# Three more waits between the four gathers of a group in a graph network's edge loop

## The reference

```python
h = x @ W1 + b1
m = relu(concat([h[dst], h[src] - h[dst]]) @ W2 + b2)
m = relu(m @ W3 + b3)
x = layernorm(x + relu(segment_max(m, dst)))
msgs = edge_weight[:, None] * x[src]
x = layernorm(x + segment_sum(msgs, dst) @ W.T + b)
```

## Time and profile before

| what | value |
|---|---|
| median of 3 runs | 2713.13 us (2711.83 to 2724.68) |
| the profiled execution | 2716.54 us, its span 2714.8 us |
| mean granted clock of TensorE | 0.880 |
| PE, DVE, POOL, ACT busy in the span | 2111.0, 1614.8, 1355.9, 824.2 us |
| DMA queue of POOL (q0) | 53312 packets, 138.17 MB |
| gathers of q rows | 784, 827.7 us busy on POOL, 478.4 us idle before them |

### The profile page before, as it was taken

One profiled execution on the slowest core, in us unless ns is written; L12 is line 12 of the kernel. 1 busy time (PEld: TensorE's weight loads), 2 busy tenths in 40 slices (PEclk: granted clock), 3 DMA queues, 4 the chain that ended last, 5 costly groups with the idle time before them and its releaser, 6 DMA issues.

```text
span 2714.8 us, 61794 instructions
## 1 busy us (share of the span) xinstructions
PE 2111.0 (78%) x15960; PEld 1850.6 (68%) x15960; DVE 1614.8 (59%) x4239; ACT 824.2 (30%) x2385; POOL 1355.9 (50%) x1300
## 2 busy tenths in 40 slices
PE   5526877777777777777785289999999999889995
PEld 5425656556565555555563289898989888888885
DVE  3326666666666666666679444443444444789997
ACT  1222223223233232232232144444545445000003
POOL 6435666666666666666634335555556555100000
PEclk7767888888888888888887599999999999999998
DMA  3224555555555555555552166666666666788885
GB/s 111 84 79 128 145 146 141 143 147 142 137 144 141 142 147 142 144 144 144 144 140 79 27 191 206 203 203 210 201 202 208 207 204 208 234 252 247 251 252 171
DMA packets 534340, 447.34 MB, mean 165 GB/s; under 512 B 64731, under 2 KB 499383, under 8 KB 534240
## 3 DMA queue, kind: packets, MB, share of 16 engines
q1 hardware_dynamic: 342788, 208.10, 28.0%
q0 software_dynamic: 53312, 138.17, 16.3%
q10 hardware_dynamic: 138140, 100.06, 12.7%
HBM read 300.43 MB, written 145.64 MB: 164 GB/s over the span
## 4 chain that ended last, share of the span: by engine, by line
PE 61%; another core or an unknown queue 17%; issue 10%; DVE 5%; ACT 3%; DVEq 2%; POOL 1%; DMA 1%; SPq 0%; ACTq 0%; POOLq 0%
PE z_ps L1426 10%; PE t_ps L1426 10%; PE z_ps L1351 6%; PE m_ps L1339 6%; PE z_ps L1450 5%; PE m_ps L1338 5%; PE m_ps L1450 4%; PE s_ps L1414 3%; PE t_ps L1360 3%; PE t_ps L1450 2%; PE s_ps L1318 1%; POOL whole L420 1%; PE s_ps L1317 1%; DVEq L1156 1%
## 5 line engine op out<-in xcount | busy, mean ns | idle before, releaser
L414 POOL DMA_INDIRECT whole<-q_tab,src_ti x784 | 827.7, 1056 | 478.4 <-issue 197.2
L430 POOL DMA_INDIRECT tab<-whole,row_at x392 | 420.3, 1072 | 373.7 <-ACT whole L688 183.2
L1097 DVE TENSOR_SCALAR whole<-row_bc,node_id 128x768 f32<-128x768 uint8 x392 | 229.7, 627 | 366.8 <-remote 123.9
L1338 PE MATMUL m_ps<-ident,whole 128*128 128x128 f32 x1568 | 337.3, 300 | 19.1 <-DMA win<-p_tab 12.6
L1339 PE MATMUL m_ps<-oh,win 128*128 128x128 f32 x1568 | 328.5, 293 | 4.4 <-issue 4.1
L1426 PE MATMUL t_ps<-win,whole 128*128 128x128 f32 x2352 | 305.3, 286 | 21.3 <-issue 17.2
L1426 PE MATMUL z_ps<-win,whole 128*128 128x128 f32 x2352 | 300.6, 284 | 19.9 <-issue 8.6
L1426 PEld LDWEIGHTS t_ps<-win,whole 128*128 128x128 f32 x2352 | 282.7, 197 | 26.7 <-issue 20.6
L1145 DVE SCALAR_TENSOR_TENSOR whole<-iota_f,scratch,whole 128x384 f32<-128x384 f32 x440 | 269.5, 613 | 45.9 <-PE m_ps L1450 34.8
L1426 PEld LDWEIGHTS z_ps<-win,whole 128*128 128x128 f32 x2352 | 278.6, 195 | 26.2 <-issue 20.0
L1338 PEld LDWEIGHTS m_ps<-ident,whole 128*128 128x128 f32 x1568 | 272.9, 218 | 21.1 <-issue 21.0
(11 more groups left out here) (270 smaller groups left out, 3104.3 us busy)
## 6 DMA issues: line engine op xcount, KB each, us to landing
win<-p_tab SPq DMA_DIRECT2D x784, 64.0 KB
seg_tab<-run_e ACTq DMA_DIRECT2D x196, 256.0 KB
win<-xw_tab SPq DMA_DIRECT2D x784, 64.0 KB
whole<-tab SPq DMA_DIRECT2D x220, 200.0 KB
whole<-tab ACTq DMA_DIRECT2D x220, 200.0 KB
row_bc<-seg_row_tab SPq DMA_DIRECT2D x196, 128.0 KB
row_bc<-rel_tab SPq DMA_DIRECT2D x196, 96.0 KB
whole<-q_tab,src_ti POOLq DMA_INDIRECT x784
```

The lines of the kernel that those rows point to most:

```text
L414: pool.indirect_dma_start(qg[:, g % RING, j, :], None, q_tab[:, :], IOA(ap=src_ti[:, t:t + 1], axis=0)).then_inc(q_ld[g % RING], 16)
L430: pool.indirect_dma_start(tab[:, :], IOA(ap=row_at[0:FR, k:k + 1], axis=0), fat[0:FR, k % RR, :], None).then_inc(fat_st[k % RR], 16)
L1097: last = V.tensor_scalar(pick[:, s, j, :], row_bc[:, r, 0:GK * SLOTS], node_id[:, j:j + 1], None, ALU.is_equal)
L1338: mm(m1_ps[:, s, c], lhsT=qg[:, r % RING, j, :], rhs=ident[:], start=True, stop=False)
```

## The change

For groups from RING + 2 = 14 on, the second, third and fourth gather of a group each wait for an event of their own: first_done of group g-11 (POOL waits for the count g - RING + 2), run_ev of group g-14 (count g - RING - 1), and run_done of group g-13 (count g - RING). The first gather waits for m1_done as before.

```diff
@@ -411,6 +411,13 @@
                     pool.wait_ge(m1_done, g - RING + 1)
                 for j in range(GT):
                     t = GT * g + j
+                    if g >= RING + 2:
+                        if j == 1:
+                            pool.wait_ge(first_done, g - RING + 2)
+                        if j == 2:
+                            pool.wait_ge(run_ev, g - RING - 1)
+                        if j == 3:
+                            pool.wait_ge(run_done, g - RING)
                     pool.indirect_dma_start(qg[:, g % RING, j, :], None, q_tab[:, :], IOA(ap=src_ti[:, t:t + 1], axis=0)).then_inc(q_ld[g % RING], 16)
```

## The result

| | before | after |
|---|---|---|
| median | 2712.48 us (2710.0 to 2724.68, 4 runs) | 2755.52 us (2746.58 to 2764.83, 4 runs) |
| ratio | | 1.0151 [1.012, 1.0182] |
| profiled execution | 2716.54 us | 2761.03 us, its span 2759.3 us |

The forecast was 2640 us, a gain of 73; it became a loss of 43, outside the range of 2560 to 2730. Lines behind the change stand seven higher in the kernel after: L414 is L421, L625 L632, L900 L907, L942 L949. In the kernels of the experiments they are shifted by each one's own edit (by three in most: L900 is L903 there, L942 L945, L973 L976).

What follows compares the result with a forecast made beforehand. The prediction took PE's signals, held while gathers are under way, to bound the first edge loop at 6.43 us a group. Spacing would save 0.41 x 182 = 75 us from 2716.5, giving 2641, stated as 2640 us; range 2560 to 2730.

Steps and rivals of the forecast that it cites:

- What bounds the loop: First edge loop: something that goes with the gathers costs 2.2 us a group, over 400 us in all.
- The rival by which nothing matters but bytes on shared DMA engines: First edge loop: events already passed or bytes under way set the hold-up, so nothing changes, 2713 us; chance 0.16.
- That PE's signal is held while gathers are under way: First edge loop: PE's signals pass before a train's data or after its last landing; waiters released 2.2 us late.
- 4 x 1.25 + 1.3 = 6.3 us: Period of a group in the first edge loop: four gather steps of 1.25 us plus 1.3 until the last has landed.
- POOL's floor: POOL's gathers in the first edge loop need 21.6 us in four groups against 25.7, a ceiling of 187 us gained.
- I take 1.65 us in four groups, 40% of it: Gain from spacing gathers in the first edge loop: 40% of the 4.1 us ceiling, 0.41 x 182 = 75 us.
- the term of 75 us: Gain expected from spaced gathers over 182 groups of the first edge loop: 0.41 us each, 75 us.
- the sign that the prediction named for this case: If right, ACT's wait before L625 would be shorter than the 1.6 us seen over one train.
- The held gather: Beside DVE's one-hot L942: gather 1, now waiting for L900, loses its 1.56 us overlap but waits as long; nothing either way.
- Rival 2: First edge loop: POOL becomes the efficient bound at 21.6 us in four groups, 2526 us; chance 0.07.
- Rival 1: First edge loop: run_ev's held signal delays gathers 2 and 3 by 1.7 us, losing 62 us, 2775 us; chance 0.22.

Runs made afterwards that it cites:

- no_gathers: Kernel before with gathers for the first 12 groups only, the rest reading the ring's old rows; 2297.21 us, ratio 0.847.
- tiny_rows: Kernel before with each gather from group 12 on fetching 4 bytes of its 128 rows instead of 512; 2708.87 us, ratio 0.9982.
- plain_loads: Kernel before with every gather of q rows replaced by a plain DMA of 128 consecutive rows, issued by SP; 2409.17 us, ratio 0.8881.
- half_gathers: Kernel before with only the first two gathers of each group issued from group 12 on; 2301.33 us, ratio 0.8601.
- spaced: Kernel before with a small iota on POOL behind each of a group's first three gathers; 2722.62 us, ratio 1.0035.
- pairs: Changed kernel with only the third gather waiting, for first_done, and no other new wait; 2714.98 us, ratio 1.001.
- w1_first: Changed kernel with only the second gather's new wait (first_done) kept; 2761.93 us, ratio 1.0178.
- w23_late: Changed kernel without the second gather's wait, keeping the third's for run_ev and the fourth's for run_done; 2734.47 us, ratio 1.007.
- w1_turn_again: Kernel before plus the second gather's wait for first_done only where g is a multiple of four (the large one-hot's step); 2786.04 us, ratio 1.0267.
- w1_turn: Kernel before plus the second gather's wait for first_done only where g is a multiple of four, batch with before at 2346.03 us; 2344.92 us, ratio 1.0.
- w1_rest: Kernel before plus the second gather's wait for first_done only where g isn't a multiple of four, batch with before at 2346.03 us; 2346.46 us, ratio 1.0.
- w3_only: Changed kernel with only the fourth gather's wait, for run_done, batch with before at 2346.03 us; 2344.24 us, ratio 0.9993.
- after_rest: Changed kernel with its three waits dropped where g is a multiple of four, batch with before at 2346.03 us; 2346.93 us, ratio 1.0002.
- two_groups: Kernel before with POOL waiting for m1_done only once for two groups, so trains of eight gathers; 2932.14 us, ratio 1.0807.
- w1_rest_again: Kernel before plus the second gather's wait for first_done only where g isn't a multiple of four; 2731.25 us, ratio 1.0076.
- after_rest_again: Changed kernel with its three waits dropped where g is a multiple of four; 2705.59 us, ratio 1.0124, in the batch with before at 2675.68 us.

## Why the prediction was wrong

**What bounds the loop** was right in the main. It was to be the gathers, at 2.2 us a group and over 400 us; no_gathers gives 415 and 4.14 us a group. That q rows aren't late, that the bytes don't count, that the tail keeps its pace and that all stages behind 1420 us stay: each was found so. The rival by which nothing matters but bytes on shared DMA engines falls with tiny_rows and plain_loads: more than a quarter of the moved bytes taken away (143 to 103 GB/s) changed 0.2% of the time. The Trainium skill (DMA: Bandwidth & Descriptors, "Issuing engines are not separate DMA queues") says that DMAs started by any engine run on the same 16 DMA engines and interleave there; nothing here speaks against that, but it prices no part of this loop.

That PE's signal is held while gathers are under way was read from one train and holds for the loop. The table gives the mean time from the end of a group's last matmul of `gathered` (or from the end of ACT's operation before, where that is later) until ACT starts relu_1, counted from the traces, 400 to 1390 us (400 to 900 for half_gathers, no_gathers and the last row); the last column is the change of the whole time.

| kernel | m1_done held, us | change against the kernel before, us |
|---|---|---|
| before | 1.09 | |
| tiny_rows | 1.24 | none |
| spaced | 1.02 | +9.5 |
| pairs | 2.38 | none |
| after | 1.82 | +43 |
| w1_first | 1.64 | +50 |
| w23_late | 2.68 | +23 |
| w1_turn_again | 1.22 | +74 |
| half_gathers | 0.14 | -374 |
| no_gathers, plain_loads | 0.06 | -415, -304 |
| w1_turn, w1_rest, w3_only, after_rest (before 2346.03 us) | 0.06 | none |

Without gathers on POOL nothing is held, nor in the batch of 2346 us, with all its gathers. But how long m1_done is held does not give the time: pairs holds it twice as long as before and loses nothing. The prediction's sum for the period, "4 x 1.25 + 1.3 = 6.3 us", fits the kernel before and not the others: spaced should have taken 2850 us by it, and two_groups, expected at 12.1 us for two groups, took 15.3.

**POOL's floor** was right too: 21.6 us in four groups were worked out, and where nothing holds POOL they took 21.8. Hence, if batches may be compared, of the 8.9 us that gathers add in four groups (25.7 against 16.8 in the tail's pace) about 5.0 are POOL's own pace and 3.9 the hold-up. The prediction took it that spacing could reach 40% of the 4.1 us up to that floor.

**The first step that failed** is "I take 1.65 us in four groups, 40% of it". It rested on the reading that a signal of PE gets through in a gap between two landings, with nothing in the trace of before that showed such a gap at work. It put m1_done 1.0 to 2.2 us sooner; in the kernel after it comes later, held for 1.82 us against 1.09. spaced has the gaps and pairs has a wait in the middle: 2722.62 and 2714.98 us, no gain, and with 0.5 us and more between the gathers of spaced m1_done is held for 1.02 us. So the term of 75 us had nothing under it. In the profile after, the sign that the prediction named for this case, a shorter wait before L625, is reversed: 417.6 us against 311.3.

**The second** is "The held gather: ... the same time is spent waiting: nothing either way". This is the dearest thing that the runs isolate. Before, POOL went into DVE's one-hot with a gather issued and came out with that gather done; the held gather was cheap because it was issued in time that nothing else could use. Waiting for an event behind the one-hot spends the same 3.1 us and issues nothing: one gather later, 1.25 us, 45 times, 56 us, and then a longer train. w1_turn_again shows it alone: 1.56 us a turn, 74 us in all, where the prediction had nothing. pairs shows that it vanishes one gather later, and w1_first that this one wait is enough for a loss of the change's size. That it makes up the 43 us of the whole change is not shown: there only 14 of 38 turns have the gap, and the waits outside the turn cost 20 us (w1_rest_again) and 30 us (after_rest_again) without it. Why they do wasn't found. The prediction had both facts on the page, L900's place behind L942 and gather 1 held for 2.51 us, and priced neither against the other.

Rival 2, POOL as an efficient bound at 2526 us, came only in the batch where nothing is held, and there without the waits as with them.

**Rival 1**, a loss at 2775 us, had the right sign and was near in size, but not by its mechanism. It put the price on run_ev, the late signal of the transposes, and on gathers 2 and 3. The waits on run_ev and run_done alone cost 23 us; the dear one was the prompt signal of DVE.

**What stays open.** The parts don't add up: turn 74, rest 20, the two together 50, the whole change 43. The counts at the one-hots show why a sum can't be expected (with waits in the rest POOL arrives at the turn another way: in 24 of 38 turns of the whole change, and in 23 of w1_first, a different gather is the held one), but no figure for it was derived. run_done alone cost 76 us in a batch where the kernel before took 2675.68, more than run_ev and run_done together in one where it took 2711.75; whether that is the batch or run_ev's effect wasn't separated. What in the chip keeps PE's signals from their waiters while gathers are under way no record shows. And no version was found that beats the kernel before.

## What to carry to other kernels

When work of a queue is made to wait for an event of another engine, look at what stands ahead of that event in that engine's order, in its worst step and not in the ordinary one: a short signal behind a long operation can take away the time in which the queue would work beside it. In this loop, held by one engine's issuing, delay by itself bought nothing; before giving up time for spacing, measure whether gaps are worth anything (a filler operation does) and what the suspected work costs at all (leave it out, then half of it). And read where in its events an engine stands: the same wait costs 74 us where POOL arrives early and nothing where it is ten groups behind.

## What the runs showed of the hardware that was not expected

- The kernel before took 2346.03, 2675.68 and about 2712 us in different batches, each time within half a per cent of its median. In the fastest batch PE's signals weren't held (0.06 us instead of 1.09) and POOL hardly paused in the kernels whose traces are kept. The kernels of one batch share a chip, but the chip's number isn't what decides: the batches of 2713.1 and 2346.03 us both have number 6 on record. What does decide wasn't settled.
- The cost of gathers isn't in proportion to them: two a group cost 0.12 us a group (in another batch), four 2.3.
- 128 descriptors of 4 bytes cost the loop as much as 128 of 512 (2708.87 against 2713.1 us).
- A gather issued beside DVE's 2.28 us one-hot ends 3.09 to 3.12 us after the one-hot's start, in all the traces looked at and whenever it was issued (so it takes from 1.8 to 3.1 us instead of 0.95). That is 0.8 us beyond the one-hot's own end. Where no further wait or operation lies between, the next gather starts at 3.40 to 3.42 us.
- Trains of eight gathers throughout cost 220 us more than before's mix of fours and eights with the same work.
